# A decoder layer on one core: 128 rows in the second score matmul of the last stage, heads innermost in its shared keys and values, and one gate minimum

## What is computed

```
gating = softmax(x @ W_gate.T)            # 16 heads
idx = argmax(gating); indicator = one_hot(idx, 16)
top1 = max(gating)
q, k, v = split(x @ W_qkv.T, 3)           # k, v: 16 heads of 16
k_shared = sum_h indicator[h] * k[h]      # 16 numbers per token
v_shared = sum_h indicator[h] * top1 * v[h]
att = softmax(causal(q_h @ k_shared.T / 4))
y_h = att @ v_shared                      # for all 16 heads
x = layernorm(x + y)
```

## Time and profile before

| | us |
|---|---|
| median of 3 runs | 382.43 (381.85 to 382.56) |
| profiled execution | 379.38 |
| its span, first to last instruction | 377.4 |
| PE busy | 336.8 (89%) |
| DVE busy | 276.1 (73%) |
| ACT busy | 226.2 (60%) |
| POOL busy | 207.2 (55%) |

### The profile page before, as it was taken

How to read it: one execution, slowest core, us unless ns; L and a number is a source line. 1 busy time by engine, 2 the same in 40 slices (tenths; PEclk the granted TensorE clock), 3 DMA queues, 4 the chain that set the end, 5 groups by cost and what they waited for, 6 DMA issues and landing times.

```text
span 377.4 us, 5876 instructions
## 1 busy us (share of the span) xinstructions
PE 336.8 (89%) x1912; PEld 261.3 (69%) x1912; DVE 276.1 (73%) x535; ACT 226.2 (60%) x703; POOL 207.2 (55%) x291
## 2 busy tenths in 40 slices
PE   1958899999999999999999998766989999999994
PEld 1755778778778788688688686543467767767673
DVE  2774966946957946957847859787779999987652
ACT  4637567566576566567566555134457777668672
POOL 0478644855825845825846815777864875802200
PEclk9969999999999999999999999895789999999996
DMA  7901000031000031000030000000000000000000
GB/s 257 343 39 56 3 28 2 1 113 56 2 28 0 3 111 56 2 30 0 0 123 1 1 2 3 0 0 0 1 3 14 2 14 17 1 16 14 0 16 28
DMA packets 5757, 13.05 MB, mean 35 GB/s; under 512 B 992, under 2 KB 3168, under 8 KB 5472
## 3 DMA queue, kind: packets, MB, share of 16 engines
q1 hardware_dynamic: 5184, 11.90, 9.1%
q10 hardware_dynamic: 544, 0.79, 0.7%
HBM read 11.63 MB, written 1.05 MB: 34 GB/s over the span
## 4 chain that ended last, share of the span: by engine, by line
PE 73%; DVE 14%; issue 6%; DMA 2%; ACT 2%; POOL 1%; SPq 1%; POOLq 0%; DVEq 0%; ACTq 0%
PE bank L480 12%; PE bank L359 11%; PE bank L390 8%; PE bank L376 7%; PE bank L639 5%; PE bank L469 5%; PE bank L586 5%; DVE toep L1032 4%; PE bank L619 3%; PE bank L458 3%; PE bank L628 3%; PE bank L620 3%; PE bank L618 2%; DMA anti<-in_anti 2%; PE bank L598 2%
## 5 line engine op out<-in xcount | busy, mean ns | idle before, releaser
L1438 POOL TENSOR_TENSOR prob<-prob,rden 128x512 f32<-128x512 f32 x32 | 33.5, 1046 | 72.7 <-DVE rden L1059 72.7
L1417 POOL TENSOR_TENSOR t_sin<-rot,sin 128x512 f32<-128x512 f32 x40 | 54.2, 1357 | 27.2 <-ACT rot L755 24.4
L779 ACT ACTIVATE prob<-bank,neg_max 128x128 f32<-128x128 f32 x128 | 45.3, 368 | 39.3 <-DVE neg_max L1052 39.2
L915 ACT ACTIVATE prob<-bank,neg_max 128x128 f32<-128x128 f32 x128 | 36.6, 371 | 14.7 <-DVE neg_max L1290 14.3
L359 PE MATMUL bank<-x_hi,w_hi 128*128 128x512 f32 x96 | 37.2, 469 | 8.8 <-ACT w_hi L736 8.3
L390 PEld LDWEIGHTS bank<-k_rope,q_rope 128*128 128x128 f32 x256 | 35.0, 200 | 10.5 <-DVE q_rope L1012 5.1
L480 PE MATMUL bank<-wo_hi,head_hi 128*128 128x256 f32 x128 | 39.4, 307 | 3.0 <-DVE head_lo L1086 3.0
L390 PE MATMUL bank<-k_rope,q_rope 128*128 128x128 f32 x256 | 35.6, 284 | 4.7 <-DVE q_rope L1012 4.7
L302 POOL TENSOR_TENSOR q_rope<-y,rot 128x128 f32<-128x128 f32 (+7 forms) x60 | 31.1, 523 | 10.3 <-ACT rot L865 10.3
L480 PE MATMUL bank<-wo_hi,head_lo 128*128 128x256 f32 x128 | 36.6, 286 | 0.0
L480 PE MATMUL bank<-wo_lo,head_hi 128*128 128x256 f32 x128 | 36.5, 285 | 0.0
(11 more groups left out here) (107 smaller groups left out, 820.1 us busy)
## 6 DMA issues: line engine op xcount, KB each, us to landing
w_raw<-in_wqkv SPq DMA_DIRECT2D x3, 768.0 KB, 5.2
toep<-in_toep SPq DMA_DIRECT2D x8, 256.0 KB, 3.0
wo_raw<-in_wo SPq DMA_DIRECT2D x4, 512.0 KB, 3.5
x_raw<-in_xt SPq DMA_DIRECT2D x2, 512.0 KB, 5.8
ctxT<-in_ctx SPq DMA_DIRECT2D x1, 1024.0 KB, 9.2
x<-in_x SPq DMA_DIRECT2D x1, 1024.0 KB, 9.4
out<-x SPq DMA_DIRECT2D x8, 128.0 KB, 1.7
wf<-in_wf SPq DMA_DIRECT2D x1, 784.0 KB, 4.5
```

The source lines that it names most:

```text
L779: last = act.activation(prob[:, k % 2, h * P:(h + 1) * P], score_bank[k % 2][:, h * P:(h + 1) * P], ACT.Exp, bias=neg_max[:, k % 2, h:h + ...
L915: last = act.activation(prob[:, c % 2, h * P:(h + 1) * P], fscore_bank[c % 2][:, h * P:(h + 1) * P], ACT.Exp, bias=neg_max[:, c % 2, h:h + 1])
L1417: pool.tensor_tensor(t_sin[:, par, :].rearrange("p (b t) -> p b t", b=BH), rot[:, par, :].rearrange("p (b t) -> p b t", b=BH), sin[:, :].u ...
L1438: pool.tensor_tensor(own, own, rden[:, k % 2, :].unsqueeze(2).to_broadcast([P, HG, P]), ALU.mult).then_inc(norm_done, 1)
```

## The change

- `fscores`: the second matmul takes all 128 rows of `qf` and of the low `kblock`, which adds the product of low query and low key.
- The weight columns of keys and values are permuted on the host from (head, feature) to (feature, head), so that `kvf_bank` and `kv_masked` hold the 16 heads innermost; `share` multiplies with `chosen` running along the innermost axis and sums over it contiguously.
- The gate is copied negated; one minimum gives the bias of the exponential and is also what `gscore` compares with. The plain maximum and its semaphore are gone. The exponential takes the scale -1.

```
-        gtop = sb("gtop", [P, 1])
...
-        kv_masked = x_raw[:, 0, :].rearrange("p (n h d) -> p n h d", n=2, h=FH)
+        kv_masked = x_raw[:, 0, :].rearrange("p (n d h) -> p n d h", n=2, h=FH)
...
                 out = fscore_bank[c % 2]
-                own = slice(CW * (c % 2), CW * (c % 2 + 1))
                 pe.matmul(out[:, :], qf[:, j, c, :], kblock[:, j, 0, :, :], start=True, stop=False)
-                pe.matmul(out[:, :], qf[own, j, c, :], kblock[own, j, 1, :, :], start=False, stop=False)
+                pe.matmul(out[:, :], qf[:, j, c, :], kblock[:, j, 1, :, :], start=False, stop=False)
...
-                act.copy(gate[:, :], tf_bank[:, D:D + FH]).then_inc(gate_done, 1)
+                act.mul(gate[:, :], tf_bank[:, D:D + FH], -1.0).then_inc(gate_done, 1)
...
-                act.activation(gexp[:, :], gate[:, :], ACT.Exp, bias=gneg[:, 0:1],
+                act.activation(gexp[:, :], gate[:, :], ACT.Exp, bias=gneg[:, 0:1], scale=-1.0,
...
-                dve.tensor_reduce(gtop[:, 0:1], gate[:, :], axis=AX.X, op=ALU.max).then_inc(gtop_done, 1)
-                dve.tensor_reduce(gneg[:, 0:1], gate[:, :], axis=AX.X, op=ALU.max, negate=True
-                                  ).then_inc(gneg_done, 1)
-                dve.wait_ge(gtop_done, b + 1)
-
-                dve.scalar_tensor_tensor(gscore[:, :], gate[:, :], gtop[:, 0:1], ties[:, :],
+                dve.tensor_reduce(gneg[:, 0:1], gate[:, :], axis=AX.X, op=ALU.min).then_inc(gneg_done, 1)
+                dve.wait_ge(gneg_done, b + 1)
+
+                dve.scalar_tensor_tensor(gscore[:, :], gate[:, :], gneg[:, 0:1], ties[:, :],
                                          ALU.is_equal, ALU.mult).then_inc(gscore_done, 1)
...
                 dve.tensor_tensor(kv_masked[:, :, :, :],
-                                  kvf_bank[:, :].rearrange("p (n h d) -> p n h d", n=2, h=FH),
-                                  chosen[:, :].unsqueeze(1).unsqueeze(3).to_broadcast([P, 2, FH, FD]),
+                                  kvf_bank[:, :].rearrange("p (n d h) -> p n d h", n=2, h=FH),
+                                  chosen[:, :].unsqueeze(1).unsqueeze(2).to_broadcast([P, 2, FD, FH]),
                                   ALU.mult).then_inc(masked_done, 1)
...
-                dve.tensor_reduce(kv_shared[:, :, :],
-                                  kv_masked[:, :, :, :].rearrange("p n h d -> p n d h"),
-                                  axis=AX.X, op=ALU.add).then_inc(shared_done, 1)
+                dve.tensor_reduce(kv_shared[:, :, :], kv_masked[:, :, :, :], axis=AX.X, op=ALU.add).then_inc(shared_done, 1)
...
-    wf = np.concatenate([np.asarray(a["L0_ffn_W_qkv"]), np.asarray(a["L0_ffn_W_gate"])], axis=0)
+    qkv = np.asarray(a["L0_ffn_W_qkv"])
+    shared = qkv[D:].reshape(2, FH, FD, D).transpose(0, 2, 1, 3).reshape(2 * D, D)
+    wf = np.concatenate([qkv[:D], shared, np.asarray(a["L0_ffn_W_gate"])], axis=0)
```

More of the change, by code:

```diff
@@ L220, in decoder_kernel @@
         qf_lo_done = sem("qf_lo_done")
-        gtop_done = sem("gtop_done")
         gneg_done = sem("gneg_done")
```

## The result

| | before | after |
|---|---|---|
| median of the runs shown, us | 382.14 (379.32 to 382.56) | 370.52 (370.24 to 371.69) |
| profiled execution | 379.38 | 370.43 |
| span | 377.4 | 368.5 |
| mean granted clock | 0.955 | 0.968 |

The ratio is 0.972, with a 95% interval of 0.967 to 0.977; 376.0 had meant 0.983. Two later measurements of the changed kernel, on two chips, gave 0.978 (0.974 to 0.983) and 0.976 (0.970 to 0.981).

What follows compares the result with a forecast made beforehand. DVE was taken to pace the steady blocks, PE just behind, with PE leading the tail's chain. Terms 0.87 + 3.0 + 2.9 - 0.4 = 6.4 us, off the median 382.43, gave 376.0; 8-in-10 range 373.0 to 379.6.

Steps and rivals of the forecast that it cites:

- The emptying of the array at 64 rows: Second score matmul in fscores: its weight load waits at 64 rows; with 128 rows each call saves 0.31 us.
- Rival 1: Second score matmul: the weight load still waits with 128 rows, only the sum's 2.9 us remain, 379.5; chance 0.12.
- The sum: Reduction L1277 in all eight blocks: contiguous reading takes 675 ns instead of 1036, 0.36 us per block, 2.9 in all.
- rival 2: Reduction L1277: the step is not its cost or the new layout is not faster, 378.9; chance 0.07.
- The gate: Gating on DVE: one reduction of 160 ns goes, but gscore never waited for it; worth 0, bounds 0 and 0.08 per block.
- Steady blocks: Blocks 0 to 3, about 283 to 330 us: DVE sets the pace, rows gain 0, the sum 0.36 us per block.
- Rival 3: Steady blocks: PE turns out to set the pace, 4 x 0.88 us more gained, 372.5; chance 0.04.
- Rivals 4 and 5: Clock falls in two or three steady blocks, 379, chance 0.12; clock stays low for whole blocks, slower, 386, chance 0.04.
- The tail: Blocks 4 to 7, 330 to 370 us: eleven calls at 0.31 us on the chain, 3.0 taken, plus the sum's savings.
- The passage: From attention to the last stage, about 246 to 283 us: 0.87 us from the rows, plus the sum for shares 0 and 1.
- the clock's term: TensorE's granted clock: -0.4 us, between +1.6 for an earlier return in the passage and -2.5 for two steady-block falls.
- the difference carried from the profile to the median: Profiled execution 379.38 us stood 3.05 below the runs' median 382.43; the forecast carried this difference over to the changed kernel.

## Why the prediction was right and wrong

- **The emptying of the array at 64 rows**, 0.31 us per call: right in place, a little large. A call went from 0.98 to 0.70 or 0.72, so 0.26 to 0.28. What the rows show is when the second load starts; that the array is emptied at the change is the reading of it. Rival 1, by the row groups of the Trainium skill, TensorE: Matmul & The Clock Gate, Part 3 (Packing small matmuls), fell: same rows twice, and the second load ran under the first matmul. The mask's matmul follows at 0.24 to 0.25, so the switch from fp32r to bf16 costs at most 0.02.
- **The sum**: 0.35 us each for 0.36. Right; rival 2 fell.
- **The gate**: 0. Right by the stages, in the profile after and with the gate alone.
- **Steady blocks**: right in place; 0.27 per block (0.80 over three) for 0.36. A part of the rest is the value's scaling, which takes 0.42 us there where it took 0.34. The reading that DVE sets the pace and PE is only just behind was closer than I had put it: PE was behind by 0.1 us, and the layout without the rows would have earned 0.05, not 0.36. Hiding the rows' 1.24 us per block at a worth of 0 was true of the rows alone, but their absence would have cost the layout nearly everything. Rival 3 (PE paces) is half in this. Rivals 4 and 5 did not occur in the changed kernel: PE's load waits 0.46 us at L568 and not 1.1, the rest of its new time stands elsewhere (PE is busy 12.34 of 13.00 us), and the clock stayed full. With the rows alone it did fall in one steady block.
- **The tail**: 3.53 for 4.08. Mis-sized by half a microsecond, in the rows: they alone gave 2.53 for 3.0, and eleven calls at 0.27 less the 0.41 that the forecast gave back make 2.56.
- **The passage**: 2.45 for 1.59. In product(0) to (1) the sum gave 0.32 and the two calls 0.75, as forecast (0.36 and 0.76). But the clock came back earlier, under the projection at 261 us (0.69 us less up to product(1)) and before the one at 276 us (1.81 us for 3.07). Against that stands the new stall of 2.15 us.
- **That the stages give 6.78 us where the terms summed to 6.75 is partly luck**: the passage gained 0.86 more than forecast, with the clock's help, and the steady blocks and the tail 0.83 less.
- **The step that failed is the clock's term, and with it the difference carried from the profile to the median.** The median came out 5.5 us under 376.0. About 2.5 us of it lie in the profiled pair, 8.95 us apart where the sum had 6.4. I had put the clock at -0.4, between +1.6 for the passage and -2.5 for falls in steady blocks, and at nothing elsewhere. The profiles show 2.1 us outside all that the change touches, 1.56 of them a low stretch at 237 us that is absent after. The other 3.0 us are the 3.05 by which the profile of before stood under its median: I added them to the forecast as if the changed kernel had to have the same difference, but its profiled run (370.43) was its typical one (370.52). A single profile, in the faster part of its runs, had hidden how much clock the kernel before usually loses. The runs show it: the medians of the three pairs stand 8.2 to 11.6 us apart at unequal clocks (0.955 before and 0.967 after in the middle), and 6.9 us with the 31 extra matmuls in both, at about 0.967 in both.

**Shown**: the worth of the parts in the steady blocks and the tail, where the clock is full; the interaction of rows and layout; that low stretches of 3.4 to 10.2 us come and go between executions of one kernel, and that where PE leads the chain one of 3.4 us cost 1.6 or 1.7 and one of 6.8 us some 3.2. **Not settled**: why the changed kernel keeps its clock better, whether because of what its PE stream does or because its work falls differently in time. That it does is in the runs (median clock 0.967 over 16 runs, against 0.955 over 75 of before). Its recorded PE busy share is not higher (88% against 89%). The gate alone, with the PE work of before, had 0.962 to 0.966 in four of six runs and won 1%, and extra PE work in the kernel before raised its clock and won nothing.

## What to carry to other kernels

Where two engines are both nearly full in a steady loop, price an edit on one together with an edit on the other: each alone may be worth nothing, and both together up to the smaller of the two savings. Try the same number of rows in neighbouring matmuls, even if that means computing terms that aren't needed: here the 64 rows left out had cost 0.26 to 0.28 us per call. Where stretches of low clock are in the profile, ask for several executions before the sum is set against a median, and give the clock a range of several microseconds either way; a part measured alone by its time has that noise in it, so read its stages too.

## What was not expected of the hardware

- Low-clock stretches came in places where PE is recorded as busy, and differed between executions of one kernel. The changed kernel had one of 3.4 us at 269.7 us in one profile and one of 10.2 us at 269.6 in another, 3.1 us slower there. The Trainium skill, TensorE: Matmul & The Clock Gate, Part 1, has the clock follow how busy PE has been; that extra work took away the stretches at 237 and at 252 to 254 us agrees, but with 31 matmuls one came at 272 us instead.
- A DVE operation from SBUF to SBUF can be held for some 2 us by a run of POOL products (2.15 us for a copy of 128 elements, 1.68 for a scaling of 16), while in the same run of products the reduction L1272 took its usual 0.69. A shorter hold, 1.02 us for a norm application of 0.40, is in every steady block.
- `gscore` started 0.19 or 0.20 us after whichever reduction came first, one or two of them.
